# Expert rows scattered while the attention runs, then loaded plainly in tiles of 122

## The reference, cut to what matters

```python
cap = math.ceil(T / E * CAP_FACTOR)          # 8192 / 12 * 1.25 -> 854
rw, sel = jax.lax.top_k(probs, TOP_K); rw = rw / rw.sum(axis=-1, keepdims=True)
# per expert e
mask = sel.T == e                            # first choices of all tokens, then second ones
pos = jnp.cumsum(mask.ravel()) - 1           # the place; from 854 on it is dropped
xs = x[tok]                                  # x: the layer-normalised rows
h = jax.nn.silu(xs @ we1.T * (xs @ we3.T)) @ we2.T
# all experts
out = zeros.at[toks].add(h * w[:, None])     # added to the residual x
```

## Time and profile before

| | us |
|---|---|
| median of 3 runs | 2416.98 |
| the profiled execution, its own time | 2416.92 |
| its span, first to last instruction | 2415.2 |
| attention stage, to the last table scatter | 2110 |
| last table scatter to the end | 305 |

### The profile page before, as it was taken

The page is one execution under the profiler, slowest core; times in us unless marked ns, Lnnn a source line. Parts: engine busy times, 40 slices in busy tenths (PEclk is TensorE's granted clock), DMA queues, the critical chain, the costliest instruction groups (busy, mean ns, idle before and its releaser), DMA issues. The chain is left out here.

```text
span 2415.2 us, 54028 instructions
## 1 busy us (share of the span) xinstructions
PE 2254.9 (93%) x13058; PEld 1145.1 (47%) x13058; DVE 1876.5 (78%) x5286; ACT 1774.2 (73%) x6911; POOL 1096.9 (45%) x1943
## 2 busy tenths in 40 slices
PE   3899999999999999999999999999999999577992
PEld 1345555555555555555555555555555555244550
DVE  5878888888888888888888888888888887545662
ACT  5878788888888888788888888888788887334541
POOL 4434444444444444444444444444444443368875
PEclk9899999999999999999999999999999999878985
DMA  8577766677766777667677767777766776369997
GB/s 252 101 158 145 142 140 140 138 139 143 147 140 143 143 144 141 141 140 140 138 139 143 148 139 143 143 141 142 143 140 140 138 140 126 79 163 189 188 171 94
DMA packets 892480, 347.98 MB, mean 144 GB/s; under 512 B 827115, under 2 KB 827371, under 8 KB 892399
## 3 DMA queue, kind: packets, MB, share of 16 engines
q1 hardware_dynamic: 865822, 296.93, 60.9%
q0 software_dynamic: 22912, 43.15, 9.8%
q10 hardware_dynamic: 3696, 7.34, 0.9%
HBM read 91.20 MB, written 57.63 MB: 62 GB/s over the span
## 5 line engine op out<-in xcount | busy, mean ns | idle before, releaser
L753 PE MATMUL pb<-wo,o 128*128 128x512 f16 x3072 | 711.0, 381 | 15.5 <-DVE o L1011 13.6
L885 ACT ACTIVATE work<-pb,small 128x128 f32<-128x128 f32 x1024 | 455.2, 453 | 174.8 <-DVE small L1074 174.0
L1345 POOL TENSOR_TENSOR small<-small 128x4 f32<-128x4 f32 (+1 forms) x584 | 485.8, 835 | 54.0 <-POOL small L1416 13.8
L1416 POOL TENSOR_TENSOR small<-small 128x4 f32<-128x4 f32 x256 | 84.2, 329 | 878.1 <-ACT junk_q L866 878.1
L753 PEld LDWEIGHTS pb<-wo,o 128*128 128x128 f16 x3072 | 287.2, 98 | 348.3 <-DVE o L1011 18.2
L684 PE MATMUL pb<-wq,xT 128*128 128x512 f16 x1536 | 356.6, 382 | 1.0 <-DVE q L1062 1.0
L684 PE MATMUL pb<-wq,wkv_raw 128*128 128x512 f16 x1536 | 352.4, 379 | 0.7 <-DVE q L1062 0.7
L1062 DVE SCALAR_TENSOR_TENSOR q<-pb,small,q 128x128 f16<-128x128 f32 x1024 | 288.3, 344 | 73.6 <-ACT q L875 73.5
L875 ACT ACTIVATE q<-pb,small 128x128 f16<-128x128 f32 x1024 | 291.1, 366 | 7.2 <-DMA qT<-q 7.2
L866 ACT ACTIVATE junk_q<-pb 128x128 bf16<-128x128 f32 x1024 | 273.4, 305 | 6.7 <-PE pb L684 6.6
L899 ACT ACTIVATE o<-pb 128x512 f16<-128x512 f32 x256 | 153.6, 600 | 138.6 <-PE pb L741 133.3
(11 more groups left out here) (154 smaller groups left out, 3481.8 us busy)
## 6 DMA issues: line engine op xcount, KB each, us to landing
work<-x SPq DMA_DIRECT2D x128, 256.0 KB, 3.1
work<-c SPq DMA_DIRECT2D x64, 256.0 KB, 3.9
out<-work SPq DMA_DIRECT2D x64, 256.0 KB, 2.0
xn_scratch<-work SPq DMA_DIRECT2D x64, 256.0 KB, 2.3
wo_raw<-wo ACTq DMA_DIRECT2D x4, 1024.0 KB, 9.2
qT<-q SPq DMA_TRANSPOSE x256
pT<-p SPq DMA_TRANSPOSE x256
wq_raw<-wq ACTq DMA_DIRECT2D x3, 1024.0 KB, 11.3
```

Source lines behind the costliest of these rows:

```text
L753: mm = nc.tensor.matmul(WO_B[:, :], o16[:, HPG * a + h, :], part(O0 + g, b_)[:, h, :], start=(g == 0 and h == 0 and n == 0), stop=(g == NG ...
L885: ex = nc.scalar.activation(probs[:, cols], S_B[:, cols], ACT.Exp, bias=nmax[:, h:h + 1], scale=esc, accum_out=psums[:, h:h + 1])
L1345: return nc.gpsimd.tensor_tensor(out_, in_, neghalf[:, 0:n], ALU.pow)
```

## The change

`norm2` writes its rows into one of two new buffers `xn2[par]` (in the raw weights' space), no longer in place. The store of `xn2_scratch` is gone. Instead POOL writes each block's 128 rows of 2 KB twice, to the places of its first and of its second expert in a DRAM tensor `expert_rows`, with two indirect DMAs per block behind the table scatter; a destination past the capacity is skipped. In the expert stage the 84 gathers are gone: SP loads the 854 rows of an expert with one plain DMA, 122 partitions of 7 rows of 2 KB each, into one of four `xg` buffers. DVE bounds the loaded rows to -32..32 (a place that was never written could hold anything). All tiles and halves of the expert stage are 122 rows or multiples of that (halves of 488 and 366 columns). The memsets of `xg` and of `lists` are gone.

```diff
+                def scatter_rows(b, par):
+                    wait_apart(pool, (dst_rdy, b + 1), (n_lo, b + 1), (s_rows, 32 * b))
+                    for k in range(2):
+                        nc.gpsimd.indirect_dma_start(
+                            out=rows_d, out_offset=bass.IndirectOffsetOnAxis(ap=dst[:, k:k + 1], axis=0),
+                            in_=xn2[par], in_offset=None, bounds_check=ROWS - 1,
+                            oob_is_err=False).then_inc(s_rows, 16)
...
@@ POOL body
+                        if g == 1 and live(b - 3):
+                            scatter_rows(b - 3, 1 - par)
...
@@ norm2, place
-                    wait(dve, d_x1, 16 * (b + 1))
-                    nc.vector.tensor_scalar(x_res, x_res, mv_2[:, 0:1], rstd_2, ALU.subtract,
+                    wait(dve, s_rows, 32 * (b - 1))
+                    nc.vector.tensor_scalar(xn2[par], x_res, mv_2[:, 0:1], rstd_2, ALU.subtract,
...
                     wait(dve, s_table, 32 * b)
+                    wait(dve, s_rows, 32 * b)
...
@@ SP body
-                        if g == 3 and live(b - 1):
-                            store_xn2(b - 1)
...
@@ experts, SP
+            def load_rows(e):
+                wait(sp, tr_done, NT * (e - NX + 1))
+                sp.dma_start(xg[e % NX][0:P], rows_d[e * CP:e * CP + CAP, :].rearrange(
+                    "(p t) n -> p t n", t=NT)).then_inc(d_g[e % NX], 16)
+            sp.wait_ge(s_rows, 32 * NB)
+            for e in range(NX):
+                load_rows(e)
             for e in range(2, E):
...
                 sp.dma_start(w13_s[i], w13[e]).then_inc(d_w13[i], 16)
+                if e + 2 >= NX and e + 2 < E:
+                    load_rows(e + 2)
...
@@ experts, POOL: gather() and its calls go; the adds are of 122 rows
-                        out=out, out_offset=bass.IndirectOffsetOnAxis(ap=lists[:, e, t, 0:1], axis=0),
-                        in_=yb[i][:, t, :], in_offset=None, compute_op=ALU.add).then_inc(d_add[i], 16)
+                        out=out, out_offset=bass.IndirectOffsetOnAxis(ap=lists[0:P, e, t, 0:1], axis=0),
+                        in_=yb[i][0:P, t, :], in_offset=None, compute_op=ALU.add).then_inc(d_add[i], 16)
...
@@ experts, DVE
+            def bound_rows(e):
+                dve.wait_ge(d_g[e % NX], 16 * (e // NX + 1))
+                nc.vector.tensor_scalar(xg[e % NX][0:P], xg[e % NX][0:P], -ROW_MAX, ROW_MAX, ALU.max,
+                                        ALU.min).then_inc(cl_done, 1)
```

More of the change, by code:

```diff
@@ L35, in experts @@
     ACT = mybir.ActivationFunctionType
-    wait, wait_apart, sem, pb, ident, xn2_d, s_z, d_lists, d_w13, d_w2, xg, w13_s, w2_s, lists = (gt[k] for k in (
-        "wait", "wait_apart", "sem", "pb", "ident", "xn2_d", "s_z", "d_lists", "d_w13", "d_w2", "xg", "w13_s", "w2_s",
+    wait, wait_apart, sem, pb, ident, rows_d, s_rows, d_lists, d_w13, d_w2, xg, w13_s, w2_s, lists = (gt[k] for k in (
+        "wait", "wait_apart", "sem", "pb", "ident", "rows_d", "s_rows", "d_lists", "d_w13", "d_w2", "xg", "w13_s", "w2_s",
         "lists"))
@@ L83, in _, with scatter_add @@
         def _(pool):
[L84 to L95, removed]
+            def scatter_add(e):
+                j, i = e // 2, e % 2
+                lists_in(pool, e)
                 wait_apart(pool, (d_add[1 - i], 16 * NT * (j + i)))
@@ L102, in scatter_add @@
                     nc.gpsimd.indirect_dma_start(
-                        out=out, out_offset=bass.IndirectOffsetOnAxis(ap=lists[:, e, t, 0:1], axis=0),
-                        in_=yb[i][:, t, :], in_offset=None, compute_op=ALU.add).then_inc(d_add[i], 16)
[L107 to L119, removed]
+                        out=out, out_offset=bass.IndirectOffsetOnAxis(ap=lists[0:P, e, t, 0:1], axis=0),
+                        in_=yb[i][0:P, t, :], in_offset=None, compute_op=ALU.add).then_inc(d_add[i], 16)
+            for e in range(E):
+                scatter_add(e)
             for i in range(2):
@@ L158, in down @@
                         pe.wait_ge(yev_done[1 - p], CNT[1 - p] * e + (t - 3) // 2 + 1)
[L159 to L163, removed]
+                    cols = slice(t * P, (t + 1) * P)
+                    pe.wait_ge(hl_done, 2 * e + (1 if t < H0 else 2))
+                    nc.tensor.matmul(Y_B[t % 3][0:P, :], h_parts[:, cols], w2_hi[:, :], start=True, stop=False)
+                    nc.tensor.matmul(Y_B[t % 3][0:P, :], h_parts[0:F, cols], w2_lo[:, :],
                                      start=False, stop=True).then_inc(y_done[p], 1)
@@ L367, in build @@
         w2_s = [wo_raw[:, 1, i, :] for i in range(2)]
+        xn2 = [wkv_raw[:, 1, i, :] for i in range(2)]
         lists = wkv_raw[:, 0, NC - 1, 0:2 * E * NT].bitcast(i32).rearrange("p (e t o) -> p e t o", e=E, o=2)
@@ L1311, in body @@
                         if g == 3 and live(b - 1):
-                            norm2(b - 1)
+                            norm2(b - 1, 1 - par)
                         if g == 3 and live(b + 2):
@@ L1510, in body @@
                             root_total(b + 1)
-                        if g == 0 and isinstance(b, int) and b == 2:
+                        if g == 1 and isinstance(b, int) and b == 3:
                             pool.wait_ge(d_sent, 32)
[L1513 to L1516, removed]
                         if g == 1 and live(b - 3):
@@ L1538, in body @@
                             rms_q(*far)
-                        if isinstance(b, int) and (b, g) in ((NB - 1, 3), (NB, 1)):
-                            nc.gpsimd.memset(xg[0 if b < NB else 1], 0.0).then_inc(s_z, 1)
+                        if g == 1 and live(b - 3):
+                            scatter_rows(b - 3, 1 - par)
                 loop(pool, body)
                 pool.wait_ge(s_table, 32 * NB)
-        experts(nc, gt=dict(wait=wait, wait_apart=wait_apart, sem=sem, pb=pb, ident=ident, xn2_d=xn2_d, s_z=s_z,
+                pool.wait_ge(s_rows, 32 * NB)
+        experts(nc, gt=dict(wait=wait, wait_apart=wait_apart, sem=sem, pb=pb, ident=ident, rows_d=rows_d, s_rows=s_rows,
                             d_lists=d_lists, d_w13=d_w13, d_w2=d_w2, xg=xg, w13_s=w13_s, w2_s=w2_s, lists=lists),
```

64 lines of the change are left out of this document (33 added, 31 removed).

## The result

The changed kernel took 2915.06 us (median of 4 runs, 2910.05 to 2917.18), the kernel before on the same chip 2415.81 (4 runs, 2411.84 to 2418.34). The ratio is 1.206, interval 1.2048 to 1.2078: 20.6% slower. The forecast was 2745, its range 2600 to 2850. So the sign was right and the size too small: 499 us more than before where 328 were forecast, and outside the range.

What follows compares the result with a forecast made beforehand. Bound: PE in attention; POOL's gathers and adds, 22.5 us an expert. Forecast: 2116.3 to first load + 420 loads + 14 weights + 121 adds + 72 tail = 2743 us span, so 2745 us (13.6% slower), range 2600 to 2850.

Steps and rivals of the forecast that it cites:

- Attention: Attention blocks: two more indirect DMAs, 2.7 us of POOL each block, are covered; POOL, DMA and DVE cost 0.
- The load: Expert stage: a row load of 122 partitions uses 2 of 16 engines and takes 35 us, range 24 to 36.6.
- DVE's bound: Expert stage: bounding the loaded rows adds 2.5 to 3.8 us on DVE, which stays under 20 of 50 us.
- What lies behind the load: Expert stage: loads follow each other at 35 us; ten experts' weights add 14 us, nine experts' adds 121 us.
- PE, ACT, DVE, POOL: all hidden: Expert stage: these engines have 17 to 18 us of work an expert and get 50 us.
- The second rival: Expert stage: adds of 122 rows are narrow too, up to 60 us an expert; 2828 us in all, chance 0.13.
- The tail: After the last load: weights, up projection, first tile down, then the adds of experts 9, 10 and 11; 72 us.
- The queue never runs dry: Expert stage: row loads are issued early enough that all 12 follow each other, 12 x 35 = 420 us.
- the adds' part in the load's engines: Expert stage: adds beside loads add up fully, 13.5 us an expert, 121 us for experts 0 to 8.
- First: Expert stage: the load uses all 16 engines and takes 4.6 us; 2389 us in all, chance 0.09.
- Third: Expert stage: the load is narrow but adds cost it nothing; 2745 - 121 = 2624 us, chance 0.13.
- Fourth: Attention: row scatters hold up `rms_q` by 2.7 us a block, 173 us more; 2918 us, chance 0.02.

Runs made afterwards that it cites:

- adds_124: wide_both with only its adds changed, to 124 rows instead of 128: 2530.6 us, ratio 1.047 to the kernel before.
- adds_126: wide_both with only its adds changed, to 126 rows instead of 128: 2404.3 us, ratio 0.996 to the kernel before.
- wide_adds: The changed kernel with adds of 128 rows and lists loaded 128 wide, row loads still 122 partitions: 2677.6 us, ratio 1.108 to the kernel before.
- wide_both: The changed kernel with row loads split into 112 and 10 partitions, lists 128 wide and adds of 128 rows: 2396.12 us, ratio 0.991 to the kernel before.

## Why the prediction was right and where it failed

**Attention: right.** Cost 0 for POOL, DMA and DVE: PE's time in the block is unchanged, and loads start at 2116.68 where 2116.3 was forecast. A row scatter took 0.98 us in the median (0.97 to 1.08), where a gather's 1.08 was put down.

**The load: right.** Two of 16 engines, read off the quotient of two rows of lists, was the step that gave the sign: 12.7% of the engines, 33 us a load. The Trainium skill's sentence that went against it (page "DMA: Bandwidth & Descriptors", section "Bandwidth": batches of 1 MiB and more reach 75% of the peak or more), measured at 128 partitions, does not carry over to 122: 1.75 MB moved at 54 GB/s.

**DVE's bound: right** in being hidden, 2.03 us where 2.5 to 3.8 were put down; leaving it out changed nothing.

**What lies behind the load: this is the step that failed**, in its sentence on the adds: "14.2 an expert, 13.5 with 122 rows". It took an add of 122 rows for 122/128 of one of 128. The diff narrows the adds by the same number that had just been found to narrow the load, and the step carried the rule over only in a rival, with 0.13, as no row showed an indirect DMA of such a width. Three costs came of it.

- *POOL.* "PE, ACT, DVE, POOL: all hidden" had the issue of an add at 1.54 us; it is 2.93, and it goes with the entries of an add, 976 in place of 128. Seven adds take 22.3 us where they took 12.6. Neither forecast nor rival had this.
- *The landing.* Alone it is 14.9 us after the last issue. The second rival had 15.4 us for an add on two engines and said that an expert would take up to 60 us beside loads: measured 57 to 66. In `adds_124` and `adds_126` it goes with the divisor, as that rival's rule says (the Trainium skill, same page, section "Why a DMA increments its semaphore by 16 and not by 1": the largest number up to 16 that divides the slowest dimension). Here the trace agrees, for software-generated transfers also: an add of 126 rows has 16 x 9 entries and one of 124 rows 16 x 31. The rival priced rows only, not the empty entries on the other engines.
- *The first adds.* 157 us between expert 0's and expert 1's, in no case of the prediction. Entries that move nothing wait for their turn on the two engines that load, one for each run of 14 KB; with 2 KB runs the gap is 22.8.

**The tail** shows the sum's error in one place. The loads were through at 2643, 28 us earlier than the 2671 that the forecast's terms add up to (2116.3 + 420 + 14 + 121). But it took for granted that adds keep up with loads, so that three experts' were left (72 us). Expert 5's were only starting at 2645.03: seven experts' were left, 269 us from 2643 to the end. 28 less and 197 more are the whole miss of 169 us. The loads set the pace in the forecast; in the kernel the adds did. "The queue never runs dry" failed with it: the row loads of experts 8 to 11 were issued 57 to 64 us apart, one for each round of the adds, at 33 us a load, and from 2399 to 2409 the queue of the loads moved nothing.

**A second term was mis-sized** with no effect on the sign: the adds' part in the load's engines is 9 to 10 us, not 13.5. `wide_adds`, the forecast case proper, takes 2677.6 and not 2745.

**The rivals.** First: not what the changed kernel does, but its number was good: 2389 against 2396.1 with the widths mended. In part that is luck: its sum takes 18.6 us an expert, though it names 19.5 as the largest (which gives 2399), and `wide_both` has 19.8 in the mean. Second: right in mechanism and nearest, 2828 against 2915.1, but its nearness hides misses that cancel. It had nine periods of 60 us beside loads; the kernel had one of 199.1 (139 more), four of 57 to 66 (5 more), and then four of 37 to 40 after the loads had ended (87 less); start and end add 27. Third: not seen, since adds cost the loads 9 to 10 us an expert in `wide_adds`. Fourth: not seen; its 2918 is next to the measured 2915.1 by chance, for the attention did not pay.

## What to carry to other kernels

Give every DMA, plain or indirect, a count of partitions (or of rows) that is a multiple of 16, or at least one with a large divisor up to 16 (126 rows cost 8 us where 127 cost 790): 122 costs 233 us in the adds and 281 in the loads here, and sentinel rows or a split into 112 + 10 give it back. When a width is found to be bad for one transfer of a change, cost every other transfer that the change gives this width by the same rule. And work moved off an engine is worth only what the next chain leaves: 9.2 us of gathers an expert went from POOL, and 21 to 28 us in all came back, since PE was already busy 167 of 190 us in that stage and the DMA share was 0.92.

## What the runs showed of the hardware that was not expected

- An indirect DMA of a poor row count costs GpSimd too: 1.54, 1.58, 2.19, 2.93 and 4.68 us for 128, 126, 124, 122 and 127 rows. The 6944 packets of seven adds hold 854 rows.
- Empty entries are not free: the last 485 took 91 us beside loads in runs of 14 KB. Beside a row load alone each run lets one entry pass, 37 and 37 in 10 us with 14 KB, 236 and 236 with 2 KB.
- With 127 rows GpSimd stands still 23 to 28 us after the fourth add of an expert (35 in the first).
- Runs of 14 KB on 16 engines moved 227 GB/s where runs of 2 KB moved 284, at a DMA share of about 1 in both; on two engines 54 and 50.
- The issue on SP can take long. In the changed kernel the two loads of `w2T` held SP for 46.65 us at 2210.70, where they take about 1.1 us in `wide_both`. The row loads in front of them were still in flight; that SP waited for room in their queue is argued, not shown:

```profile
2210.70 46.65 SPq L94 DMA_DIRECT2D wo_raw<-w2T  x2
```
